# Filling the score stack of a cross-attention with four transfers instead of twelve, and issuing its shift rows from Pool

## What is computed

```python
k, v = split((ctx @ W_src.T + b_src) * mask)          # 8 heads of 32
q = (layernorm(x) @ W_tgt.T + b_tgt) * mask
scores = einsum('bthd,bshd->bhts', q, k) / sqrt(32)
scores = where(mask == 0, -inf, scores)
update = einsum('bhts,bshd->bthd', softmax(scores), v)
x = x + tanh(g) * (concat([layernorm(x), update]) @ W_out.T + b_out)
```

## Time and profile before

| | |
|---|---|
| median of 3 runs | 688.38 us |
| lowest, highest | 686.52, 689.06 us |
| the profiled execution's own time | 686.24 us |
| its span | 684.2 us |
| mean granted TensorE clock | 0.995 of full speed |
| busy in the span | PE 643.1, DVE 430.1, ACT 425.4, Pool 201.3 us |
| stage C | from about 257 to 584 us |

### The profile page before, as it was taken

One profiled execution on the slowest core, in us unless ns is written; L12 is line 12 of the kernel. 1 busy time (PEld: TensorE's weight loads), 2 busy tenths in 40 slices (PEclk: granted clock), 3 DMA queues, 4 the chain that ended last, 5 costly groups with the idle time before them and its releaser, 6 DMA issues.

```text
span 684.2 us, 10968 instructions
## 1 busy us (share of the span) xinstructions
PE 643.1 (94%) x3497; PEld 439.2 (64%) x3497; DVE 430.1 (63%) x982; ACT 425.4 (62%) x1149; POOL 201.3 (29%) x299
## 2 busy tenths in 40 slices
PE   5988899999999998699999999999999987899997
PEld 3754555555543357588878777887887865556654
DVE  7973847776776648477667666666566686152522
ACT  7766655535544433587777778777777777545452
POOL 6574424210110012133444332323332220242110
PEclk9999999999999999999999999999999999999999
DMA  8821116501000005543433554434345440001112
GB/s 276 246 98 62 62 32 260 85 1 62 0 1 1 0 0 127 127 94 99 117 94 99 126 125 99 116 99 113 100 100 126 94 95 2 1 17 45 56 38 92
DMA packets 43130, 58.01 MB, mean 85 GB/s; under 512 B 13152, under 2 KB 24002, under 8 KB 42818
## 3 DMA queue, kind: packets, MB, share of 16 engines
q1 hardware_dynamic: 43074, 57.33, 30.9%
HBM read 27.46 MB, written 4.19 MB: 46 GB/s over the span
## 4 chain that ended last, share of the span: by engine, by line
PE 64%; SPq 15%; DMA 6%; DVE 4%; POOL 4%; issue 3%; ACT 3%; DVEq 0%; POOLq 0%; ACTq 0%
SPq L513 13%; PE bank L1147 12%; PE bank L1159 6%; DMA c_stack<-neg_row 5%; PE bank L1567 4%; PE bank L1362 4%; PE bank L1432 4%; PE bank L1371 4%; PE bank L1385 3%; PE bank L1408 3%; PE bank L1344 3%; PE bank L1557 3%; PE bank L1123 3%; SPq L528 2%; PE bank L1558 2%
## 5 line engine op out<-in xcount | busy, mean ns | idle before, releaser
L936 ACT ACTIVATE c_junk<-bank,c_nmx 128x256 bf16<-128x256 f32 x256 | 117.2, 484 | 15.5 <-DVE c_nmx L1894 15.3
L1894 DVE TENSOR_REDUCE c_nmx<-bank 128x4 f32<-128x1024 f32 x64 | 75.3, 1218 | 38.5 <-PE bank L1385 38.5
L1147 PE MATMUL bank<-b_o,cw 128*128 128x512 f32 x192 | 90.6, 603 | 1.8 <-ACT b_o L804 1.8
L780 ACT ACTIVATE b_h<-bank,cb 128x512 f32<-128x512 f32 x48 | 32.8, 686 | 51.0 <-PE bank L1147 51.0
L958 ACT ACTIVATE c_pT<-bank 128x1024 f32<-128x1024 f32 x64 | 61.6, 1013 | 4.3 <-PE bank L1408 4.3
L1046 ACT ACTIVATE d_h<-bank,b_col 128x512 f32<-128x512 f32 x64 | 39.6, 686 | 39.4 <-PE bank L1558 39.4
L1147 PEld LDWEIGHTS bank<-b_o,cw 128*128 128x128 f32 x192 | 34.5, 190 | 44.9 <-issue 41.1
L1344 PE MATMUL bank<-c_ctxT,wsrcT 128*128 128x256 f32 x256 | 61.5, 385 | 0.4 <-DVE c_vb L1886 0.4
L1362 PE MATMUL bank<-wsrcT,c_ctxT 128*128 128x256 f32 x240 | 56.7, 379 | 0.0
L936 ACT ACTIVATION_READ_ACCUMULATOR c_junk<-bank,c_nmx 128x1 f32 x256 | 55.6, 217 | 0.0
L1408 PE MATMUL bank<-c_stack 99*128 99x256 f32 x256 | 46.9, 313 | 7.8 <-DMA c_stack<-c_rows 7.6
(11 more groups left out here) (190 smaller groups left out, 1289.3 us busy)
## 6 DMA issues: line engine op xcount, KB each, us to landing
c_stack<-c_parts SPq DMA_DIRECT2D x192, 128.0 KB
a_ctx<-in_ctx SPq DMA_DIRECT2D x16, 512.0 KB, 4.0
c_ctxT<-turned_ctx SPq DMA_DIRECT2D x16, 512.0 KB, 4.3
out_x<-x_sb SPq DMA_DIRECT2D x7, 512.0 KB, 2.9
x_sb<-in_x SPq DMA_DIRECT2D x3, 1024.0 KB, 11.2
mask_b<-in_mask_BxS_fk SPq DMA_DIRECT2D x1, 2048.0 KB, 11.6
x_sb<-in_x SPq DMA_DIRECT2D x2, 512.0 KB, 5.4
wsrcT<-turned_w_src SPq DMA_DIRECT2D x1, 1024.0 KB, 5.8
```

Source lines behind the costliest of these rows:

```text
L936: op = nc.scalar.activation(c_junk[:, tc, j, :], scores(tc)[:, j, :], ACT.Exp, bias=c_nmx[hg][:, tc, j:j + 1], accum_out=c_sum[hg][:, tc, ...
L1147: op = mm(bank[2 * u + h][:], cw1[:, c, h * P:(h + 1) * P], b_o[n % LANES][:, c, :], start=c == 0, stop=c == DK - 1)
L1894: v.tensor_reduce(c_nmx[hg][:, tc, :], scores(tc), AXIS.X, ALU.max, negate=True)\
```

## The change

Heads stand side by side in the channels: the weights and biases of q and k are permuted on the host, so that partition 4d + j of `c_parts` is feature d of head j (it was 32j + d). One transfer of all 128 partitions then fills a half of a third for all four heads. The parts are reordered so that two of them that belong to one third are neighbours; two of the three thirds take one transfer for q and k together, the first third takes two. The stack's columns are ordered head, half, group, token. The mask row is written from a source row of 512 tokens (`neg_rows`, loaded by two transfers instead of one) in four pieces instead of eight. The biases of q and k come as contiguous columns.

The shift rows are issued by Pool on its own queue. Pool's order for a batch becomes: rows of b-1, group 1; `split_q`; `bias_c`; rows of b, group 0; then as before.

```diff
-Q_LO, Q_HI, K_HI, K_LO = range(PARTS)
+Q_LO, K_HI, Q_HI, K_LO = range(PARTS)
-STACK_DMAS = 3 * QH + 1
+STACK_DMAS = 4 + 1
...
-            def stack_c(b, s, thirds):
+            def stack_c(b, s):
                 if b == 1:
                     sp.wait_ge(b_ok[3], 2 * PAIRS)
                 need(sp, c_k_split, 2 * b + 2)
-                need(sp, c_qlo_ok, b + 1)
                 need(sp, c_sT_ps, 2 * TS * (b - 1))
...
-                for c in thirds:
-                    first, step = ((Q_HI, K_HI - Q_HI), (Q_LO, K_HI - Q_LO), (Q_HI, K_LO - Q_HI))[c]
-                    for j in range(QH):
-                        sp.dma_start(
-                            c_stack[s][c * HD:(c + 1) * HD, :, j, :, :].rearrange("p a g t -> p a (g t)").bitcast(F32),
-                            c_parts[j * HD:(j + 1) * HD, first:first + step + 1:step, :, :]
-                            .rearrange("p a g t -> p a (g t)").bitcast(F32)).then_inc(c_stack_in, 16)
+                need(sp, c_qlo_ok, b + 1)
+                for c, a, part, count in ((0, 1, K_HI, 1), (0, 0, Q_HI, 1), (1, 0, Q_LO, 2), (2, 0, Q_HI, 2)):
+                    sp.dma_start(
+                        c_stack[s][c * HD:(c + 1) * HD, :, a:a + count, :, :].rearrange("p j a g t -> p j (a g t)").bitcast(F32),
+                        c_parts[:, part:part + count, :, :].rearrange("p a g t -> p (a g t)").bitcast(F32))\
+                        .then_inc(c_stack_in, 16)
...
             for b in range(B):
-                if b > 0:
-                    rows_c(b - 1, 1 - b % 2, 1)
                 if b + 1 < B:
-                    stack_c(b + 1, 1 - b % 2, (0, 1))
-                rows_c(b, b % 2, 0)
-                if b + 1 < B:
-                    stack_c(b + 1, 1 - b % 2, (2,))
+                    stack_c(b + 1, 1 - b % 2)
                     masks_c(b + 1, 1 - b % 2)
                 if b + 3 < B:
                     stream_c(b + 3, 1 - b % 2)
-            rows_c(B - 1, 1, 1)
...
+            def rows_c(b, s, hg):
+                pool.wait_ge(c_rows_ok, 2 * b + hg + 1)
+                for tc in range(TS):
+                    nc.gpsimd.dma_start(
+                        c_stack[s][MASK_ROW + 1:MASK_ROW + 1 + SHIFTS, :, 0, hg, tc * P:(tc + 1) * P].bitcast(F32),
+                        c_rows[hg][tc * SHIFTS * QH:(tc + 1) * SHIFTS * QH, :].bitcast(F32)).then_inc(c_rows_in, 16)
+
             def body_c(b, s):
+                if not is_first(b):
+                    rows_c(b - 1, 1 - s, 1)
                 if not is_last(b, B):
                     split_q(b + 1)
                     bias_c(b + 1)
+                rows_c(b, s, 0)
                 if not is_first(b):
                     next_stats(b - 1, 1 - s, TS, n_mv[1 - s], n_tmp[1 - s], c_nstat, c_npre, c_next, b)
...
             over_batches(body_c)
+            rows_c(B - 1, 1, 1)
```

More of the change, by code:

```diff
@@ L174, in build @@
           w_src, b_src, w_tgt, b_tgt, w_out, b_out, u1, v1, b1, u2, v2, b2,
-          ctx_turned, w_src_turned, w_tgt_turned, w_out_turned, out):
+          ctx_turned, w_src_turned, w_tgt_turned, w_out_turned, b_k_column, b_q_column, out):
     x_dram = x.rearrange("b (k p) d -> b p k d", p=P)
@@ L214, in build @@
         bq_col = sb("bq_col", [P, DK])
-        neg_row = sb("neg_row", [B, S])
+        neg_rows = sb("neg_rows", [B, DK * S])
         u1_sb = sb("u1_sb", [P, DK, RANK])
@@ L274, in build @@
             b_t1 = [sb(f"b_t1{u}", [P, GROUP], F32, st) for u in range(2)]
-            sb("b_gap", [P, 6 * KB // 4], F32, st)
+            sb("b_gap", [P, 4 * KB // 4], F32, st)
+            ginit_b = sb("ginit_b", [P, D], F32, st)
+            bin_b = sb("bin_b", [P, D], F32, st)
             a_xs = [sb(f"a_xs{s}", [P, TS, D], F32, st) for s in range(2)]
@@ L302, in build @@
             winT = sb("winT", [P, DK, D], F32, st)
-            ginit_b = sb("ginit_b", [P, D], F32, st)
-            bin_b = sb("bin_b", [P, D], F32, st)
         with ExitStack() as st:
@@ L319, in build @@
             c_upT = [sb(f"c_upT{s}", [P, DK, S], F32, st) for s in range(2)]
-            c_stack = [None, sb("c_stack1", [MASK_ROW + 1 + SHIFTS, 2, QH, DK, S], F32R, st)]
-            c_stack[0] = sb("c_stack0", [MASK_ROW + 1 + SHIFTS, 2, QH, DK, S], F32R, st)
-            sb("c_third", [P, 2 * TS * DC], F32, st)
+            c_stack = [None, sb("c_stack1", [MASK_ROW + 1 + SHIFTS, QH, 2, DK, S], F32R, st)]
+            c_stack[0] = sb("c_stack0", [MASK_ROW + 1 + SHIFTS, QH, 2, DK, S], F32R, st)
+            sb("c_third", [P, 2 * TS * DC - KB // 4], F32, st)
             c_ctxT = [sb(f"c_ctxT{s}", [P, FK, S], F32, st) for s in range(2)]
@@ L421, in build @@
             (wsrcT[:], w_src_turned), (wtgtT[:], w_tgt_turned), (woutT[:], w_out_turned),
-            (bk_col[:], column(b_src[0:D])), (bq_col[:], column(b_tgt)),
+            (bk_col[:], b_k_column), (bq_col[:], b_q_column),
             (mask_b[:], mask.partition_broadcast(P)),
-            (mask_col[:], mask.rearrange("b (k p) -> p b k", p=P)), (neg_row[:], mask),
+            (mask_col[:], mask.rearrange("b (k p) -> p b k", p=P)), (neg_rows[:, 0:S], mask), (neg_rows[:, S:DK * S], mask),
             (bout_b[:], row_on_all(b_out)), (b2_b[:], row_on_all(b2)), (bv_b[:], row_on_all(b_src[D:2 * D])),
@@ L501, in stack_c @@
                 need(sp, c_k_split, 2 * b + 2)
-                need(sp, c_qlo_ok, b + 1)
                 need(sp, c_sT_ps, 2 * TS * (b - 1))
-                if b < 2 and 0 in thirds:
+                if b < 2:
                     sp.wait_ge(s_onerow, 1)
                     sp.dma_start(c_stack[s][MASK_ROW:MASK_ROW + 1 + SHIFTS, :, :, :, :]
-                                 .rearrange("p a j g (k t) -> p (a j g k) t", t=P).bitcast(F32),
+                                 .rearrange("p j a g (k t) -> p (j a g k) t", t=P).bitcast(F32),
                                  one_rows[:].unsqueeze(1).to_broadcast([1 + SHIFTS, 2 * QH * DK * TS, P]))\
                         .then_inc(s_ones, 16)
-                for c in thirds:
-                    first, step = ((Q_HI, K_HI - Q_HI), (Q_LO, K_HI - Q_LO), (Q_HI, K_LO - Q_HI))[c]
-                    for j in range(QH):
-                        sp.dma_start(
-                            c_stack[s][c * HD:(c + 1) * HD, :, j, :, :].rearrange("p a g t -> p a (g t)").bitcast(F32),
-                            c_parts[j * HD:(j + 1) * HD, first:first + step + 1:step, :, :]
-                            .rearrange("p a g t -> p a (g t)").bitcast(F32)).then_inc(c_stack_in, 16)
+                need(sp, c_qlo_ok, b + 1)
[4 more added lines that the diff above has]
+                        .then_inc(c_stack_in, 16)
             def masks_c(b, s):
@@ L521, in masks_c @@
                 sp.dma_start(
[L522 to L530, removed]
+                    c_stack[s][MASK_ROW:MASK_ROW + 1, :, 1, :, :].rearrange("p j g t -> p j (g t)").bitcast(F32),
+                    neg_rows[b:b + 1, :].unsqueeze(1).to_broadcast([1, QH, DK * S])).then_inc(c_stack_in, 16)
             stream_c(0, 0)
@@ L534, in _ @@
             sp.wait_ge(s_neg, 1)
-            stack_c(0, 0, range(3))
+            stack_c(0, 0)
             masks_c(0, 0)
@@ L1384, in scores_c @@
                     for j in range(QH):
-                        op = mm(scores(tc)[:, j, :], c_stack[s][0:MASK_ROW + 1, 0, j, hg, tc * P:(tc + 1) * P],
-                                c_stack[s][0:MASK_ROW + 1, 1, j, hg, :], start=True, stop=True)
+                        op = mm(scores(tc)[:, j, :], c_stack[s][0:MASK_ROW + 1, j, 0, hg, tc * P:(tc + 1) * P],
+                                c_stack[s][0:MASK_ROW + 1, j, 1, hg, :], start=True, stop=True)
                     op.then_inc(c_s_ps, 1)
@@ L1407, in scoresT_c @@
                 for j in range(QH):
-                    op = mm(scores(q)[:, j, :], c_stack[s][rows, 1, j, hg, q * P:(q + 1) * P],
-                            c_stack[s][rows, 0, j, hg, :], start=True, stop=True)
+                    op = mm(scores(q)[:, j, :], c_stack[s][rows, j, 1, hg, q * P:(q + 1) * P],
+                            c_stack[s][rows, j, 0, hg, :], start=True, stop=True)
                 op.then_inc(c_sT_ps, 1)
@@ L1729, in constants_c @@
                 dve.wait_ge(s_wc, 16 * len(loads_c))
-                v.tensor_scalar(neg_row[:], neg_row[:], 0.0, MASKED, ALU.is_equal, ALU.mult).then_inc(s_neg, 1)
+                v.tensor_scalar(neg_rows[:], neg_rows[:], 0.0, MASKED, ALU.is_equal, ALU.mult).then_inc(s_neg, 1)
                 v.tensor_scalar(wtgtT[:], wtgtT[:], SCALE, None, ALU.mult).then_inc(s_wq, 1)
@@ L2054, in features_first, with heads_side_by_side, columns @@
         return np.ascontiguousarray(np.swapaxes(a, -3, -2))
+    def heads_side_by_side(a):
+        a = np.asarray(a)
+        return np.swapaxes(a.reshape((DK, QH, HD) + a.shape[1:]), 1, 2).reshape(a.shape)
+    def columns(a):
+        return np.ascontiguousarray(heads_side_by_side(a).reshape(DK, P).T)
```

(8 more changed lines are left out.)

## The result

The changed kernel takes 859.7 us (median of 4 runs, 858.7 to 860.8) against 688.1 (4 runs): ratio 1.250, 95% interval 1.247 to 1.253. The prediction had the sign right and missed the size by a factor of more than thirty: 5 us forecast, 172 measured, far outside 683 to 712.

A forecast was written before the change was run, and what follows sets the result against it. PE's work, 19.22 us a batch, was taken as the bound. Won 1.2 + 4.5 + 2.6 + 1.0 = 9.3, lost 3.6 + 6.8 + 3.8 + 1.4 = 15.6, net 6.3 slower: 693 us, range 683 to 712.

The forecast's parts named there:

- The waits for the mask row after the first batch: First scores on PE: the faster stack removes these waits, 3.6 us mid-stage and 0.89 before 563.82, 4.5 won in all.
- 1.57 MB at 200 GB/s with the DMA engines 0.87 busy, 230 GB/s if full: Stack transfers: bytes set the end, 6.8 us; the stack stands at about 424, PE asks at 427; first batch wins 1.2.
- the four transfers do not land sooner: Rival on the stack: at two thirds of today's rate, 4.5 and 1.2 stay unwon, 12 slower, 698 us; chance 0.06.
- Pool is free then, 3.2 is under 3.7, nothing lost.: Shift rows of group 0: the pair takes 3.2 us against 3.7 us of slack before PE uses them, so no loss.
- landing on Pool's queue is slow too: Rival on group 0's rows: they meet the whole stack's backlog in the DMA engines; 30.8 slower, 717 us; chance 0.18.
- x = 4.2: Upper end for Pool's first issue of a pair to both landed: 1.27 us an issue, 1.64 to land.
- x = 3.2: Forecast time from Pool's first issue of a pair to both landed: 1.0 us an issue, 1.16 to land.
- the quick rival: Transposed scores of group 1: Pool's pair as quick as SP's or quicker, 683 or 678 us; chance 0.30.
- The plain batches of group 1: Batches 0 and 6 to 13: the pair takes 3.2 us against 2.8 of slack, 3.6 us lost over nine batches.
- batches 1 to 4: Group 1, where Pool's statistics follow `split_k`: slack 1.5 us, 1.7 lost in each, 6.8 together.
- batch 5: Group 1: the weight split on Pool delays the issue to 0.6 us too late; 3.8 us lost.
- A hold of DVE on Pool: Rival in batches 1 to 4: Pool's second issue stands still while DVE normalises x, 1.0 us more each, 696.5 us; chance 0.06.

The follow-up runs named there:

- Run 1: Only the shift rows moved to Pool, against the kernel before, its twelve transfers issued by SP without a break: 687.3 us, ratio 0.9985.
- run 9: Kernel before with twelve transfers, rows on Pool, and Pool's late statistics and weight split put behind the rows of group 1: 682.2 us, ratio 0.993.
- Run 4: The change's layout, but twelve transfers, one per head and third, from 32 source partitions in steps of four to 32 destination partitions: 725.2 us.
- run 6: The change with the stack spread over 128 partitions, each third written to every fourth partition, on the source's own partitions; results not the kernel's: 699.8 us.

## Why the prediction was wrong

**The sign was luck.** The prediction made the kernel slower by what the rows cost on Pool. Run 1 has the rows on Pool with the old transfers, and comes out at 0.9985, no difference. What made the kernel slower stood in the sum at nothing, or as a win.

**The bound and what can be won.** Right: PE's work of 19.2 us a batch is the floor; where rows and stack are in time (run 9) exactly that remains, and the win is a few us. The waits for the mask row after the first batch went away as forecast (4.0 us, forecast 4.5); but they are gone in run 1 too, with twelve transfers, so that win came from taking the rows out of SP's program and not from the four transfers.

**The stack: the step that failed first.** "1.57 MB at 200 GB/s with the DMA engines 0.87 busy, 230 GB/s if full" took the rate of the old transfers for the new ones. It was some 118, and the first scores, counted as 1.2 us won, lost 6.7. The rival "the four transfers do not land sooner" set the price at two thirds of the rate and gave it 0.06, on the ground that "the reads spread over more" partitions. Run 4 shows that a spread source was no help into 32 neighbouring partitions (145 instead of 212), and run 6 that the same source is fast into other partitions (354 and more): the pairing counts, not the spread of the reads by itself. The Trainium skill, "DMA: Bandwidth & Descriptors", section "Rules for kernel authors", advises 128 partitions and few large transfers for bandwidth. The trace differs for this copy within SBUF: four transfers that read 128 partitions and write 32 moved 118 GB/s, twelve of 32 partitions 212. The measurement decides.

**Group 0: the step that failed most.** "Pool is free then, 3.2 is under 3.7, nothing lost." Pool was free and issued in time; a pair took 12.2 us from its first issue (443.02) to landing instead of 3.2, and 12.2 less the slack of 3.7 is the wait of 8.5. The rival "landing on Pool's queue is slow too" had the mechanism, rows that meet the whole backlog, and priced it at x = 4.2, because its end came from the mask row's landing, 1.64 us, behind what was left of a stack that SP issues slowly. It should have been priced by the backlog: bytes queued divided by the rate. Even at the assumed 230 GB/s that is 6.8 us from 416, and the rows were due at 422.7. The two rivals were taken as alternatives, though the one's rate sets the other's wait. The Trainium skill, "DMA: Bandwidth & Descriptors", section "Queues, rings and completion order", says that an engine takes turns between its queues packet by packet, with 9 to 17 descriptors as a typical packet and 64 as the most. By the typical figure the rows would have had their turn sooner: in the change 365 records of SP's queue, some 23 for each of 16 engines, began before the first of Pool's. If a record is a descriptor, the figure for the most would still allow it.

**Pool's price.** x = 3.2 was too high. On engines that are not backed up a pair takes 2.3 us (run 1), less than SP's 2.53; the quick rival held there. The plain batches of group 1 have no wait, batches 1 to 4 had 0.5 in run 1 (1.7 forecast), batch 5 2.5 (3.8 forecast). The places were right, the size was off. A hold of DVE on Pool of 1.0 us is not seen: Pool's 64 issues in run 1 took 0.54 to 0.80 us, median 0.55, the ten beside DVE's normalising of x among them.

**The clock** was left out of the losing side. After the waits of 8 us, matmuls at the lower level (granted 0.50) cost 44.5 us more, a quarter of the loss; the earlier trace rows had shown the same after a wait of 4.76.

## What to carry to other kernels

The rate of the copy within SBUF depended here on which partitions it reads for those it writes; a rate read from one pairing need not hold for another, so measure it before you merge transfers. A queue that is limited by issuing leaves little unmoved in front of small urgent transfers (0.14 to 0.27 MB in run 1); issuing faster than the engines move puts a backlog there (1.03 MB in the change), whichever queue the small ones come from. Price an urgent transfer by the bytes that will be queued ahead of it, and when two rivals lie on one path, price them together.

## What the runs showed that was not expected

Four transfers of the same bytes ran at 118, 160 to 245, or 354 to 392 GB/s, with the engines full each time, by the destination's partitions alone. Four large transfers moved the stack at little more than half the rate of twelve small ones. Rows of 4 KB on queues of their own, Pool's and ACT's, did not begin to move until the stack that was queued before them had. And Pool's issue, 0.55 us, is no longer than SP's (0.60 for a stack transfer before).
